# Decoder layer on one core: contiguous feed-forward weight pieces, the first layer norm's turned rows made by GpSimd from group 4 on, and orders set anew

## What is computed

```python
x = x + linear_attention(layernorm(x))          # q, k, v, o projections 256x256, 16 heads, causal, phi = elu + 1
x = x + cross_attention(layernorm(x), ctx)      # softmax, 16 heads of 16, no output projection
h = silu(tlin(n, w1)) * tlin(n, w2)             # n = layernorm(x); 256 -> 1024, weights in {-1, 0, 1}
h = gelu(tlin(h, h1)); h = gelu(tlin(h, h2))    # 1024 -> 1024, twice
x = x + tlin(h, w3)                             # 1024 -> 256
```

## Time and profile before

| | |
|---|---|
| median of 3 runs | 1068.17 us (1066.75 to 1068.72) |
| the profiled execution's own time | 1067.3 us |
| its span in the trace | 1065.5 us |
| busy: TensorE, VectorE, ScalarE, GpSimd | 1041.3, 769.4, 527.6, 262.1 us |
| matrix instructions in the trace | 10186 |
| moved by DMA | 174.87 MB, mean 164 GB/s |
| TensorE's granted clock | 1.00 in every stretch |

### The profile page before, as it was taken

The page is one execution under the profiler, slowest core; times in us unless marked ns, Lnnn a source line. Parts: engine busy times, 40 slices in busy tenths (PEclk is TensorE's granted clock), DMA queues, the critical chain, the costliest instruction groups (busy, mean ns, idle before and its releaser), DMA issues.

```text
span 1065.5 us, 25693 instructions
## 1 busy us (share of the span) xinstructions
PE 1041.3 (98%) x10186; PEld 866.9 (81%) x10186; DVE 769.4 (72%) x1708; ACT 527.6 (50%) x855; POOL 262.1 (25%) x363
## 2 busy tenths in 40 slices
PE   7999999999999999999999999999999999999998
PEld 7989877878877888778788878787888888787886
DVE  5999998767996879867798778987678455523412
ACT  4344553855536635556454556374633635433432
POOL 3323352100441114301161111620026001500600
PEclk9999999999999999999999999999999999999999
DMA  4687766443643444534645334453364435544552
GB/s 161 230 296 244 260 225 209 159 133 105 214 149 125 139 154 144 165 124 135 192 150 169 118 107 156 157 156 115 129 209 157 144 119 199 172 146 158 180 177 80
DMA packets 76742, 174.87 MB, mean 164 GB/s; under 512 B 10960, under 2 KB 26448, under 8 KB 76624
## 3 DMA queue, kind: packets, MB, share of 16 engines
q1 hardware_dynamic: 73168, 161.70, 45.1%
q10 hardware_dynamic: 3456, 11.54, 3.8%
HBM read 145.38 MB, written 39.35 MB: 173 GB/s over the span
## 4 chain that ended last, share of the span: by engine, by line
PE 84%; DVE 10%; issue 2%; DMA 2%; POOL 0%; ACT 0%; SPq 0%; ACTq 0%; DVEq 0%; POOLq 0%
PE bank L1254 43%; PE bank L1141 8%; PE bank L1239 6%; PE bank L1274 6%; PE bank L1113 5%; PE bank L1082 5%; PE bank L1097 3%; PE bank L1087 2%; DVE hidden_full L1020 2%; PE bank L1058 2%; DVE mx L989 2%; DVE hidden_full L1023 1%; PE bank L1191 1%; PE bank L1134 1%; PE bank L1122 1%
## 5 line engine op out<-in xcount | busy, mean ns | idle before, releaser
L1254 PE MATMUL bank<-hidden_a,weight_ring 128*128 128x512 f32 x1024 | 251.3, 396 | 0.0
L1254 PE MATMUL bank<-hidden_b,weight_ring 128*128 128x512 f32 x1024 | 248.1, 395 | 0.3 <-DVE inexact_flag L1045 0.3
L1254 PEld LDWEIGHTS bank<-hidden_b,weight_ring 128*128 128x128 f32 x1024 | 187.8, 188 | 39.4 <-issue 0.8
L1254 PEld LDWEIGHTS bank<-hidden_a,weight_ring 128*128 128x128 f32 x1024 | 187.2, 188 | 40.0 <-issue 1.4
L857 ACT ACTIVATE hidden_full<-bank,columns_sb 128x512 f32<-128x512 f32 x128 | 88.2, 689 | 221.8 <-PE bank L1254 221.3
L706 POOL TENSOR_TENSOR ve<-mv,eps 128x1 f32<-128x1 f32 (+1 forms) x80 | 21.1, 264 | 474.5 <-DVE mv L872 474.5
L1239 PE MATMUL bank<-hidden_b,weight_ring 128*128 128x512 f32 x512 | 123.0, 394 | 1.4 <-DMA weight_ring<-weights_scratch 1.4
L745 POOL TENSOR_TENSOR hidden_a<-hidden_full,hidden_a 128x512 fp32r<-128x512 f32 x64 | 83.0, 1297 | 167.9 <-ACT hidden_a L852 166.7
L1239 PEld LDWEIGHTS bank<-hidden_b,weight_ring 128*128 128x128 f32 x512 | 94.2, 188 | 21.3 <-DMA weight_ring<-weights_scratch 1.8
L1028 DVE TENSOR_TENSOR hidden_a<-hidden_full,hidden_a 128x512 fp32r<-128x512 f32 x64 | 43.6, 683 | 70.8 <-ACT hidden_a L863 70.6
L989 DVE TENSOR_REDUCE mx<-bank 128x4 f32<-128x512 f32 x128 | 80.3, 678 | 16.6 <-PE bank L1141 16.3
(11 more groups left out here) (135 smaller groups left out, 1696.4 us busy)
## 6 DMA issues: line engine op xcount, KB each, us to landing
weight_ring<-weights_scratch SPq DMA_DIRECT2D x160, 512.0 KB, 3.5
weights_scratch<-in_h ACTq DMA_DIRECT2D x16, 512.0 KB, 5.0
xn3T_scratch<-hidden_b SPq DMA_DIRECT2D x16, 512.0 KB, 4.0
weight_bits<-in_h SPq DMA_DIRECT2D x32, 256.0 KB, 3.6
weight_ring<-weights_scratch SPq DMA_DIRECT2D x32, 256.0 KB, 2.8
values_scratch<-hidden_full SPq DMA_DIRECT2D x14, 512.0 KB, 4.6
xv<-values_scratch SPq DMA_DIRECT2D x14, 512.0 KB, 4.2
x_in<-in_x SPq DMA_DIRECT2D x16, 256.0 KB, 2.8
```

The source lines that it names most:

```text
L1254: mm = eng.matmul(pbank(step, g, n)[:, :], ring[:, slot, kk * P:(kk + 1) * P], src[:, part, kk, :], start=(kk == 0 and part == 0), stop=(k ...
```

## The change

1. The inputs `w12`, `h1`, `h2` and `w3` are laid out on the host as pieces, each of 128 rows that follow one another in memory. The copies, the bit loads and the general path read these. A copy of 512 KB is then one contiguous run on both sides.
2. For groups 4 to 15 (`REMADE = 4`) the first layer norm's turned rows are no longer made by VectorE and TensorE. SyncE loads the turned x (`load_xT`, a new input `xT`) over `x_in` once the statistics are taken; GpSimd writes mean and reciprocal root to a small buffer; SyncE stores it (`keep_stats1`) and loads first the means, then the roots, spread over all partitions (`load_stats1`, twice); GpSimd subtracts and multiplies (`xn1`, two steps of two instructions). ScalarE's rounded copy and VectorE's rest then read `x_in` in place of a PSUM bank. VectorE's `ln1`, and TensorE's four transposes, are gone for these groups.
3. At the start, ScalarE loads its function table before it waits for the constants, and the work on the column constants comes later: their load behind two projection weights, VectorE's three small instructions after the first `ln1`, ScalarE's one before the first `q`.
4. `LEAD`, `OFFSET`, `AT`, `FILL`, `PATIENCE` and the planner's starting times are new numbers, and so all five lists are in another order.

```diff
+    REMADE = 4
-    SPARE, PATIENCE, HOLD, MANY = 1, 14.5, 0, 3
+    SPARE, PATIENCE, HOLD, MANY = 1, 17.2, 0, 3
-    LEAD = {("gpsimd", "bias"): 18.2, ("gpsimd", "ctx"): -146.3, ("gpsimd", "gate_rest"): -222.4,
...
+    LEAD = {("gpsimd", "bias"): 282.9, ("gpsimd", "ctx"): -679.5, ("gpsimd", "gate_rest"): -407.6,
...
-    AT |= {("scalar", "copy_weights", j): 31.4 + 7.60 * j for j in range(NCH)}
-    AT |= {("sync", "load_bits", i, j): 159.9 + 15.64 * (NWB * i + j) for i in range(8) for j in range(NWB)}
+    AT |= {("scalar", "copy_weights", j): 12.9 + 10.06 * j for j in range(NCH)}
+    AT |= {("sync", "load_bits", i, j): 280.3 + 12.22 * (NWB * i + j) for i in range(8) for j in range(NWB)}
...
+            x_t = x_in[:, :, :].rearrange("p b d -> p (b d)").rearrange("p (c t) -> p c t", c=C)
...
                 def load_x(g):
-                    wait_count(eng, xn1_turned, g)
+                    if 0 < g <= REMADE:
+                        eng.wait_ge(xn1_turned, g)
+                    elif g:
+                        eng.wait_ge(xn1T_done, g)
...
-                eng.dma_start(cols[:, :], columns).then_inc(cols_loaded, 16)
                 for n, (dst, src) in enumerate(zip(whole, (wqT, wkT, wvT, xkT, xvT, woT, xqT))):
+                    if n == 2:
+                        eng.dma_start(cols[:, :], columns).then_inc(cols_loaded, 16)
...
+                    elif step == "load_xT":
+                        eng.wait_ge(LN1["mean_var"], GB * g + GB)
+                        eng.dma_start(x_t, xT.rearrange("(c p) t -> p c t", p=P)[:, :, T * g:T * g + T]).then_inc(xT_loaded, 16)
+                    elif step == "keep_stats1":
+                        eng.wait_ge(LN1["rstd"], g + 1)
+                        eng.wait_ge(mean1_copied, g - REMADE + 1)
+                        eng.dma_start(st1_d[g].rearrange("w p b -> p w b"), stats1_out[:, :, :]).then_inc(stats1_stored, 16)
+                    elif step == "load_stats1":
+                        eng.wait_ge(stats1_stored, 16 * (g - REMADE + 1))
+                        if n == 1:
+                            eng.wait_ge(xn1_centred, g - REMADE + 1)
+                        elif g > REMADE:
+                            eng.wait_ge(xn1_made, g - REMADE)
+                        eng.dma_start(stats1[:, :, :].rearrange("p s b -> p (s b)"),
+                                      st1_d[g, n].rearrange("s b -> (s b)").partition_broadcast(P)).then_inc(stats1_loaded, 16)
...
+                    elif step == "xn1":
+                        half = x_t.rearrange("p c (b s) -> p c b s", b=GB)
+                        mean_or_rstd = stats1[:, :, :].rearrange("p s b -> p b s")
+                        if n == 0:
+                            eng.wait_ge(xT_loaded, 16 * (g - REMADE + 1))
+                        eng.wait_ge(stats1_loaded, 32 * (g - REMADE) + 16 + 16 * n)
+                        for c in range(C):
+                            last = eng.tensor_tensor(half[:, c], half[:, c], mean_or_rstd, (ALU.subtract, ALU.mult)[n])
+                        last.then_inc((xn1_centred, xn1_made)[n], 1)
...
+                eng.preload_act_table(ACT.Exp)
                 eng.wait_ge(consts_loaded, 16)
-                eng.preload_act_table(ACT.Exp)
...
-                        eng.activation(xn1T[:, 0, :, :], halves(pbank(step, g)), ACT.Copy).then_inc(xn1T_hi, 1)
+                        if g < REMADE:
+                            eng.wait_ge(xn1_turned, g + 1)
+                            wait_count(eng, v_psum, g)
+                        else:
+                            eng.wait_ge(xn1_made, g - REMADE + 1)
+                            eng.wait_ge(v_psum, g)
+                        eng.activation(xn1T[:, 0, :, :], halves(pbank(step, g)) if g < REMADE else x_t, ACT.Copy).then_inc(xn1T_hi, 1)
...
-                        rest(xn1T, pbank(step, g)[:, :]).then_inc(xn1T_done, 1)
+                        rest(xn1T, pbank(step, g)[:, :] if g < REMADE else x_t.rearrange("p c t -> p (c t)")).then_inc(xn1T_done, 1)
...
-                FILL = {("ln1T", 0, 0): 24, ("q", 0, 0): 20, ("xv", 0, 0): 40, ("lin_scores", 0, 1): 20}
+                FILL = {("ln1T", 0, 0): 22, ("q", 0, 0): 14, ("lin_scores", 0, 0): 24}
...
-        "w12": np.ascontiguousarray(np.stack([w1, w2], axis=2)),
+        "w12": by_piece(np.stack([w1, w2], axis=2), 1024),
```

148 lines of the change are left out of this document (85 added, 63 removed).

## The result

| | before | changed |
|---|---|---|
| median, on one chip | 1067.46 us (1065.46 to 1068.72, 4 runs) | 1077.09 us (1073.69 to 1079.27, 4 runs) |
| ratio | | 1.0084, 95% interval 1.0061 to 1.0108 |
| profiled execution, its span | 1067.3, 1065.5 us | 1073.69, 1071.9 us |
| TensorE idle in the span | 24.2 us | 34.3 us |
| of it in mid-course | 15.2 us | 26.3 us |

A forecast was written before the change was run, and what follows sets the result against it. TensorE, busy 1041.3 of 1065.5 us, was taken as the bound, VectorE pacing 40 to 200 us. Turnings 4.2, start 1.3, spare instructions 1.4 and order 1.1 sum to 8.0 us: 1068.17 to 1060.2 us, range 1051 to 1067.

The forecast's parts named there:

- Busy time: On TensorE: busy time was to fall from 1041.3 us to near 1032 us.
- Turnings: TensorE's four transposes a group, gone in twelve groups: 4.2 us gained, 3.5 at the lower end.
- spare instructions: TensorE's spare instructions cut from 104 to 60: 1.4 us gained, between 0 and 2.9 for those beyond the start.
- order: TensorE's changes between kinds of matrix work fall from 260 to 251: 1.1 us gained, between 0 and 1.8.
- The 15.2 us of idle time in mid-course is assumed to stay.: TensorE's waits between first and last instruction: assumed unchanged in total when the gains were summed.
- rival F: On TensorE: removed work only covered other waits, so idle time grows as much; 1068 us, chance 0.06.
- Rival E: SyncE's queue blocked by the statistics' trip, ring pieces late: 1077.7 us at five exposed groups, 1088 at eight; chance 0.09.
- SyncE ... it is early. Cost 0: SyncE's 48 more issues: a group's path 15.2 us longer, hidden within its 66 us; cost 0.
- Contiguous weights: 0: Weight copies, bit loads and ring pieces: hardly in TensorE's waits, so 0, up to a gain of 1.4 us.
- Rival C: First 200 us, paced by VectorE: gains from start, spare instructions and early turnings lost; 1063.6 us, chance 0.15.
- Rival D: Groups 4 and 5, ahead of 200 us: GpSimd blocks VectorE at the shared port, 5.1 us; 1065.3 us, chance 0.06.
- Cost 0 on the path: GpSimd's 48 new instructions, 45 us: hidden as long as VectorE is not held up; cost 0.

The follow-up runs named there:

- no_trip: Changed kernel without the store and two loads of the first layer norm's statistics, GpSimd reading a constant instead: 1066.7 us, ratio 0.9999.
- pool_free: Changed kernel with all new SyncE transfers and waits kept, but GpSimd not waiting for them and computing with a constant: 1069.8 us.
- moved: one_load_old with the statistics' load issued right behind their store and GpSimd's first xn1 step put right ahead of the second: 1078.9 us.
- layout_only: Kernel before with the contiguous weight pieces alone, all lists as before: 1071.3 us, ratio 1.0050.
- padded: Kernel before with the contiguous pieces, each row 64 values longer in memory so rows no longer follow one another: 1067.2 us.
- no_trip_tiny: no_trip with GpSimd's 48 xn1 instructions cut to one column of 128: 1061.7 us, ratio 0.9956.
- memset_instead: no_trip with each of the 48 xn1 instructions replaced by three memsets that take about as long and read nothing: 1067.2 us.
- remade_none: Changed kernel with REMADE = 16, so TensorE turns all groups, keeping the new layout, start and numbers: 1099.7 us, ratio 1.0301.
- old_numbers: Changed kernel with LEAD, OFFSET, AT, FILL, PATIENCE and starting times of before, groups 4 to 15 still remade: 1104.5 us.
- one_load_old: Changed kernel with the old weight layout and one 256 KB load for means and roots together: 1068.5 us, ratio 1.0025.
- old_layout: Changed kernel with the weights laid out as before, all five lists as in the changed kernel: 1075.5 us, ratio 1.0062.

## Why the prediction was wrong

**Busy time: right.** Turnings, spare instructions and order were to take TensorE from 1041.3 to 1032 us; `no_trip`, at full clock, has 1032.2. How it splits is less sure: the spare instructions' row fell from 8.4 to 5.7 us, by 2.7 where 3.6 was taken for busy time, and that of the turnings from 10.2 to 3.0. 48 fewer turnings are there (first turning at 7.68 us, predicted 7.2; `q` at 10.05, predicted 9.7).

**The step that failed** is the last of the sum: "The 15.2 us of idle time in mid-course is assumed to stay." It became 26.3. All of rival F's and E's question was in that sentence, and it had no row behind it: TensorE's waits depend on every list, and all five were new.

**"SyncE ... it is early. Cost 0": wrong, by 10.4 us** (`no_trip`). The single steps were sized almost rightly (15.2 us in all; store 5.2 and not 3.4, loads 3.9, GpSimd's instruction 775 ns and not 942: 16.1 us), but group 5's path took 131.56 - 111.49 = 20.1 us, for the first load was issued 8 us behind the store. Even so it was in time for ScalarE at 143.82. The error is another: I asked only whether the group's result comes in time, 66 us being enough, and whether ring pieces queue behind the trip. Not asked was who stands behind `xn1` on GpSimd: `bias`, `ctx` and the other roots, each needed within a few us. An in-order engine that waits 111 us in 21 places for something early is late with what stands behind it. `pool_free` gives 7 us of the 10 back, with SyncE's waits for GpSimd among them.

**Rival E** had the right sign and the right source, a trip that blocks an in-order list, and the wrong list and victim: TensorE's waits for the ring went from 1.4 us to 0.7, and no ring piece is in the chain at 130 us. That its sum for five exposed groups, 1077.7, is near the measured 1077.1 is luck. `moved` shows the SyncE form of it.

**"Contiguous weights: 0": wrong, 5 us alone** (`layout_only`, `padded`), 2 in these lists. I looked for the copies among TensorE's waits and not at what they do to the transfers beside them.

**The clock was in no term.** Before, it is 1.00 in every stretch, so no row priced it. In the changed kernel's four runs the mean is 0.9945: 0.0055 x 1075 = 5.9 us. The ledger of the profiled execution: work saved 9.1; idle time 10.1 more; TensorE busy 5.4 longer than in `no_trip`, of which (1 - 0.997) x 1071.9 = 3.2 are the clock and 2.2 are not placed; together 6.4 us of span. The runs with lower clock make the rest of 9.6.

**Rival C** (the front gains nothing) holds so far: the front lost, even without the trip. **Rival D**: GpSimd's new instructions cost 5.0 us in the median (`no_trip_tiny` against `no_trip`), the size that D gave. D's cause was the port: whether it is that, with VectorE 6.3 us longer busy (767.4 for 761.1), or GpSimd's longer list stays open, since `memset_instead` holds VectorE up too. D's place for it, groups 4 and 5 alone, was not tested. The prediction's "Cost 0 on the path" is wrong either way. VectorE at 765 us (predicted 757) and GpSimd at 299 (307) are near.

**What stays open.** With the trip gone, GpSimd's work cut to almost nothing, and either layout, 2 to 5 us of the 9.1 saved come out as time, not 8; `no_trip` is idle 27.1 us where before has 24.2, most of it ahead of 200 us. What in the new lists causes that is not shown: `remade_none` and `old_numbers` were meant to part lists from steps, and could not. Whether lists exist for the changed steps that avoid all waits over 2 us was not tried, beyond the two moves.

## What to carry to other kernels

When work moves to an engine with time to spare, ask what stands behind each new wait in that engine's list; a step that may come 60 us later still has to be placed where its data have landed. Read the clock of every stretch as a price on waits: in this kernel, whose TensorE is 98% busy, some waits of 2 us cost themselves and 1.7 us again, and others only themselves. And lists found by search belong to one set of steps: small edits in them were worth from 10 us lost (`moved`) to 7 gained (`one_load_old` beside `old_layout`) with the same work on TensorE, so weigh an edit by TensorE's busy time and its longest waits, not by one median.

## What was not expected of the hardware

Copies of 512 KB from HBM to HBM, made contiguous, cost the kernel 5 us, with 1216 packets for 3456 on their queue; padding undid it. A store of 2 KB lands after 3.0 us at the median (`stats_scratch<-mv`, 4.7 for the three ahead of 200 us), the new one after 5.2 (5.1 for its three there), and one took 7.94 us in `moved`, with 281 GB/s moved in its first 5 us. GpSimd's 128x256 instruction took 748 ns at the median in `xn1` and 871 in `res` (`no_trip`), at the same shape; the statistics that it reads lie 8 bytes apart in the one and 16 in the other, and the operations differ too. And the granted clock fell, for some 3 us at the lower level, behind single waits of TensorE as short as 1.9 us.
